# Top-32 masks that alternate between VectorE with TensorE's count and ScalarE's Sign with row sums

## The reference, cut to what matters

```python
scores = jnp.einsum('bthd,bghd->bhtg', Q, K) / np.sqrt(DH).astype(np.float32)
scores = jnp.where(vision_mask[:, None, None, :], scores, -jnp.inf)
topv, topi = jax.lax.top_k(scores, K_TOP)          # K_TOP = 32, 4 heads
probs = jax.nn.softmax(topv, axis=-1)
attn = jnp.zeros_like(scores).at[bi, hi, ti, topi].set(probs)
attn_mean = attn.mean(axis=1)                      # mean over the 4 heads
c_t = jnp.einsum('btg,bgd->btd', attn_mean, V)
```

## Time and profile before

| what | value |
|---|---|
| median of 3 runs | 3208.37 us (3207.09 to 3212.95) |
| profiled execution, its own time | 3182.96 us |
| its span | 3181.2 us |
| busy in the span: TensorE, VectorE, ScalarE, GpSimd | 2495.6, 1834.1, 1441.4, 1016.0 us |
| mean granted TensorE clock | 0.878 |
| stage of the first batch, window 1254 to 1414 us: TensorE, VectorE, ScalarE, GpSimd busy | 108.91, 135.27, 90.80, 90.65 of 160 us |

### The profile page before, as it was taken

The page is one execution under the profiler, slowest core; times in us unless marked ns, Lnnn a source line. Parts: engine busy times, 40 slices in busy tenths (PEclk is TensorE's granted clock), DMA queues, the critical chain, the costliest instruction groups (busy, mean ns, idle before and its releaser), DMA issues.

```text
span 3181.2 us, 36641 instructions
## 1 busy us (share of the span) xinstructions
PE 2495.6 (78%) x12668; PEld 1499.0 (47%) x12668; DVE 1834.1 (58%) x4565; ACT 1441.4 (45%) x2298; POOL 1016.0 (32%) x419
## 2 busy tenths in 40 slices
PE   0466698999957996668898668898669798768799
PEld 0432232223214663455476455476456476456477
DVE  8455011121231113975896975796975787794877
ACT  3033476776831223631454641454651354551254
POOL 1022000100001112640581650591560490460392
PEclk9988798999978998588999679899679899669899
DMA  1044743334151112021000011000002000002000
GB/s 56 0 161 171 127 64 67 51 67 65 47 186 35 45 43 58 1 60 43 21 1 17 28 46 58 21 1 13 30 8 96 21 1 10 27 1 96 0 1 8
DMA packets 89044, 147.35 MB, mean 46 GB/s; under 512 B 16784, under 2 KB 59408, under 8 KB 88816
## 3 DMA queue, kind: packets, MB, share of 16 engines
q1 hardware_dynamic: 81328, 135.38, 16.2%
q0 software_dynamic: 7504, 9.35, 1.6%
HBM read 121.98 MB, written 22.88 MB: 46 GB/s over the span
## 4 chain that ended last, share of the span: by engine, by line
PE 56%; DVE 23%; issue 9%; ACT 7%; DMA 3%; SPq 1%; POOL 1%; DVEq 0%; ACTq 0%; POOLq 0%
PE ps L1651 7%; PE ps L1642 6%; PE ps L1254 4%; PE ps L1265 4%; PE ps L1629 3%; DVE sb_xnT L2241 3%; PE ps L1521 3%; ACT sb_arena L917 3%; PE ps L1591 2%; PE ps L1422 2%; PE ps L1489 2%; PE ps L1441 2%; PE ps L1435 2%; PE ps L1571 2%; PE ps L1580 2%
## 5 line engine op out<-in xcount | busy, mean ns | idle before, releaser
L917 ACT ACTIVATE sb_arena<-ps 128x1024 f32<-128x1024 f32 x416 | 403.2, 1021 | 166.1 <-PE ps L1254 163.5
L2241 DVE MAX8 sb_xnT<-sb_arena 128x8 f32<-128x60 f32 (+1 forms) x1728 | 245.7, 203 | 74.6 <-ACT sb_arena L1011 74.6
L1651 PE MATMUL ps<-sb_arena 128*128 128x512 f32 x512 | 278.7, 629 | 2.7 <-ACT sb_arena L1085 2.7
L689 POOL TENSOR_TENSOR sb_arena<-sb_arena 128x1024 f32<-128x1024 f32 x96 | 227.5, 2370 | 165.0 <-DVEq L2349 153.9
L1254 PE MATMUL ps<-sb_arena 96*128 96x512 bf16 x832 | 240.8, 397 | 47.3 <-issue 33.3
L1642 PE MATMUL ps<-sb_arena 128*128 128x64 f32 x2048 | 260.2, 271 | 0.0
L1642 PEld LDWEIGHTS ps<-sb_arena 128*128 128x128 f32 x2048 | 252.2, 194 | 0.3
L1098 ACT ACTIVATE sb_arena<-ps,sb_arena 128x512 f32<-128x512 f32 x256 | 175.6, 686 | 167.5 <-DVE sb_arena L2390 166.0
L801 POOL TENSOR_TENSOR sb_arena<-sb_arena 128x1601 f32<-128x1601 f32 x56 | 175.4, 3132 | 210.3 <-DVE sb_arena L2229 210.3
L691 POOL TENSOR_TENSOR sb_arena<-sb_arena 128x1024 f32<-128x1024 f32 x84 | 227.9, 2713 | 6.6
L1265 PE MATMUL ps<-sb_arena 128*32 128x512 f32 x1664 | 227.9, 620 | 1.5 <-ACT sb_arena L917 1.5
(11 more groups left out here) (342 smaller groups left out, 4755.9 us busy)
## 6 DMA issues: line engine op xcount, KB each, us to landing
sb_arena<-in_ctxT SPq DMA_DIRECT2D x13, 1601.0 KB, 7.3
sb_arena<-k_spill SPq DMA_DIRECT2D x96, 208.0 KB, 8.0
sb_arena<-in_dft SPq DMA_DIRECT2D x5, 2048.0 KB, 8.0
k_spill<-sb_arena SPq DMA_DIRECT2D x12, 832.0 KB, 5.2
sb_arena<-in_w SPq DMA_DIRECT2D x16, 512.0 KB, 7.2
sb_arena<-in_idft SPq DMA_DIRECT2D x4, 2048.0 KB, 9.6
sb_arena<-in_wf SPq DMA_DIRECT2D x8, 1024.0 KB, 12.9
sb_arena<-q_spill SPq DMA_DIRECT2D x96, 64.0 KB, 9.2
```

The lines of the kernel that those rows point to most:

```text
L689: link(eng.tensor_tensor(heads(tmp if e else v2[:, :, hs]), src, mix, ALU.mult))
L917: A(probs0[:, 2 * (m % 4):2 * (m % 4) + 2, :], ps[:, 2 * (m % 2):2 * (m % 2) + 2, :], ACT.Exp).then_inc(pair_probs, 1)
L1651: mm(ps[:, S2_BANKS[n % 4], :], q2z[:, h, t * P:(t + 1) * P], kT2[:, h // 2, :], start=True, stop=True).then_inc(s2_done, 1)
L2241: ins = V.max(cand[:, n % 2, 8 * j:8 * j + 8], s_sb[:, n % 6, c0:c0 + w])
```

## The change

Even items stay as they are. For odd items the mask comes from ScalarE: `Sign(score + bias)` over the 1601 scores, where the bias is minus a value just under the 32nd largest. VectorE makes this bias with three instructions on one column, and no longer compares the scores. The mask is then plus and minus one, and its row sums come out of the same instruction; TensorE sums the 128 row sums with a single 128 x 1 matmul, and ScalarE copies the one number with its sign turned. `settle` and `weight` of an odd item move from step k == 4 to step k == 6 of the next item. `scale_head` takes Relu in place of Copy, so that the negative products become zero, and the last two items' masks are clipped at zero.

```diff
-ALL_DECIDED = int(np.float32(P * TOPK).view(np.int32))
+ALL_DECIDED = [int(np.float32(P * n).view(np.int32)) for n in (TOPK, GKEYS - 2 * TOPK)]
+JUST_UNDER = 2.0 ** -22
...
 # GpSimd
                     pool.wait_ge(e1_ready, nth(b, e1_ready, n + 1))
+                    if n % 2:
+                        pool.wait_ge(sign_ready, nth(b, sign_ready, n // 2 + 1))
                     pool.wait_ge(w1_ready, nth(b, w1_ready, n + 1))
                     G.tensor_tensor(e, e, kept01[:, n % 2, 0:GKEYS], ALU.mult).then_inc(p1_kept, 1)
...
 # ScalarE
-                    A(p if n % H1 else p_mean[:, t % 2, 0:GKEYS], p, ACT.Copy, scale=stat1[:, n % 3, WEIGHT:WEIGHT + 1]).then_inc(p1_scaled, 1)
+                    A(p if n % H1 else p_mean[:, t % 2, 0:GKEYS], p, ACT.Relu, scale=stat1[:, n % 3, WEIGHT:WEIGHT + 1]).then_inc(p1_scaled, 1)
...
                     A(probs1[:, n % 3, 0:GKEYS], s_sb[:, n % 6, 0:GKEYS], ACT.Exp, bias=bias).then_inc(e1_ready, 1)
-                    act.wait_ge(count_done, nth(b, count_done, n + 1))
-                    A(kept_by_col[0:1, :], ps[0:1, 7, 3 * P:4 * P], ACT.Copy, accum_out=kept[0:1, n:n + 1]).then_inc(count_ready, 1)
-                    A(top_e[:, n % 2, :], top[:, n % 2, :], ACT.Exp, bias=bias,
-                      accum_out=stat1[:, n % 3, SUM:SUM + 1]).then_inc(sum1_ready, 1)
+                    if n % 2:
+                        if n >= 3:
+                            act.wait_ge(p1_kept, nth(b, p1_kept, n - 1))
+                        A(kept01[:, 1, 0:GKEYS], s_sb[:, n % 6, 0:GKEYS], ACT.Sign, bias=under[:, 2:3], accum_out=signs).then_inc(sign_ready, 1)
+                        A(top_e[:, n % 2, :], top[:, n % 2, :], ACT.Exp, bias=bias,
+                          accum_out=stat1[:, n % 3, SUM:SUM + 1]).then_inc(sum1_ready, 1)
+                        act.wait_ge(count_done, nth(b, count_done, n + 1))
+                        A(kept[0:1, n:n + 1], ps[0:1, 7, 3 * P:3 * P + 1], ACT.Copy, scale=-1.0).then_inc(count_ready, 1)
+                    else:
...
 # TensorE, count(n)
-                    pe.wait_ge(choice_ready, nth(b, choice_ready, n + 1))
                     if n >= 1:
                         pe.wait_ge(count_ready, nth(b, count_ready, n))
+                    if n % 2:
+                        pe.wait_ge(sign_ready, nth(b, sign_ready, n // 2 + 1))
+                        ins = mm(ps[0:1, 7, 3 * P:3 * P + 1], signs, ones[:, :], start=True, stop=True)
+                    else:
...
 # VectorE
-                    with dve.If(kept_bits != ALL_DECIDED):
+                    with dve.If(kept_bits != ALL_DECIDED[n % 2]):
...
-                        if k == 4 and n >= 1:
+                        if k == (6 if (n - 1) % 2 else 4) and n >= 1:
                             settle(n - 1)
                             weight(n - 1)
                         search(n + 1, k)
...
+                    least = eights[:, TOPK - 1:TOPK]
+                    if n % 2:
+                        if n >= 3:
+                            dve.wait_ge(sign_ready, nth(b, sign_ready, n // 2))
+                        V.tensor_scalar(st[:, NEG:NEG + 1], eights[:, 0:1], -1.0, None, ALU.mult)
+                        V.tensor_scalar(under[:, 0:1], least, JUST_UNDER - 1.0, 1.0e-30, ALU.mult, ALU.add)
+                        link(V.tensor_scalar(under[:, 1:2], least, -1.0 - JUST_UNDER, None, ALU.mult))
+                        V.tensor_scalar(under[:, 2:3], under[:, 1:2], under[:, 0:1], None, ALU.max).then_inc(top_ready, 1)
+                    else:
...
+                        V.tensor_scalar(kept01[:, 0, 0:GKEYS], s, least, None, ALU.is_ge).then_inc(choice_ready, 1)
```

More of the change, by code:

```diff
@@ L244, in program @@
         kept_by_col = at(o, [P]); o += P
+        signs = at(o, [1]); o += 1
+        under = at(o, [3]); o += 3
         probs1 = at(o, [3, KS]); o += 3 * KS
@@ L445, in program @@
         sum1_ready = sem("sum1_ready", 16)
-        choice_ready = sem("choice_ready", 16)
+        choice_ready = sem("choice_ready", 8)
+        sign_ready = sem("sign_ready", 8)
         count_ready = sem("count_ready", 16)
@@ L1046, in _ @@
                     A(probs1[:, n % 3, 0:GKEYS], s_sb[:, n % 6, 0:GKEYS], ACT.Exp, bias=bias).then_inc(e1_ready, 1)
-                    act.wait_ge(count_done, nth(b, count_done, n + 1))
-                    A(kept_by_col[0:1, :], ps[0:1, 7, 3 * P:4 * P], ACT.Copy, accum_out=kept[0:1, n:n + 1]).then_inc(count_ready, 1)
-                    A(top_e[:, n % 2, :], top[:, n % 2, :], ACT.Exp, bias=bias,
-                      accum_out=stat1[:, n % 3, SUM:SUM + 1]).then_inc(sum1_ready, 1)
+                    if n % 2:
[7 more added lines that the diff above has]
+                    else:
+                        act.wait_ge(count_done, nth(b, count_done, n + 1))
+                        A(kept_by_col[0:1, :], ps[0:1, 7, 3 * P:4 * P], ACT.Copy, accum_out=kept[0:1, n:n + 1]).then_inc(count_ready, 1)
+                        A(top_e[:, n % 2, :], top[:, n % 2, :], ACT.Exp, bias=bias,
+                          accum_out=stat1[:, n % 3, SUM:SUM + 1]).then_inc(sum1_ready, 1)
                     if 1 <= n < TILES * H1 - 1:
@@ L1495, in count @@
                 def count(n):
-                    pe.wait_ge(choice_ready, nth(b, choice_ready, n + 1))
                     if n >= 1:
                         pe.wait_ge(count_ready, nth(b, count_ready, n))
[L1500 to L1503, removed]
+                    if n % 2:
+                        pe.wait_ge(sign_ready, nth(b, sign_ready, n // 2 + 1))
+                        ins = mm(ps[0:1, 7, 3 * P:3 * P + 1], signs, ones[:, :], start=True, stop=True)
+                    else:
+                        pe.wait_ge(choice_ready, nth(b, choice_ready, n // 2 + 1))
+                        for i in range(KCH):
+                            k = -i % KCH
+                            ins = mm(ps[0:1, 7, 3 * P:3 * P + KW[k]], ones_col[:, :], kept01[:, 0, k * P:k * P + KW[k]],
+                                     start=(i == 0), stop=(i == KCH - 1))
                     ins.then_inc(count_done, 1)
@@ L2266, in _ @@
                         dve.wait_ge(p1_scaled, nth(b, p1_scaled, n - 2))
[L2267 to L2271, removed]
+                    least = eights[:, TOPK - 1:TOPK]
[7 more added lines that the diff above has]
+                    else:
+                        V.tensor_scalar(st[:, NEG:NEG + 1], eights[:, 0:1], -1.0, None, ALU.mult).then_inc(top_ready, 1)
+                        if n >= 2:
+                            dve.wait_ge(p1_kept, nth(b, p1_kept, n - 1))
+                            dve.wait_ge(count_ready, nth(b, count_ready, n - 1))
+                        V.tensor_scalar(kept01[:, 0, 0:GKEYS], s, least, None, ALU.is_ge).then_inc(choice_ready, 1)
                 mean = p_mean[:, (TILES - 1) % 2, 0:GKEYS]
@@ L2279, in _ @@
                     dve.wait_ge(e1_ready, nth(b, e1_ready, n + 1))
-                    link(V.scalar_tensor_tensor(s_cut[:, 0:GKEYS], kept01[:, n % 2, 0:GKEYS], stat1[:, n % 3, WEIGHT:WEIGHT + 1],
-                                                probs1[:, n % 3, 0:GKEYS], ALU.mult, ALU.mult))
+                    link(V.scalar_tensor_tensor(s_cut[:, 0:GKEYS], kept01[:, n % 2, 0:GKEYS], 0.0, probs1[:, n % 3, 0:GKEYS], ALU.max, ALU.mult))
                     dve.wait_ge(p1_added, nth(b, p1_added, n - TILES))
-                    V.tensor_tensor(mean, mean, s_cut[:, 0:GKEYS], ALU.add).then_inc(p1_added, 1)
+                    V.scalar_tensor_tensor(mean, s_cut[:, 0:GKEYS], stat1[:, n % 3, WEIGHT:WEIGHT + 1], mean, ALU.mult, ALU.add).then_inc(p1_added, 1)
                 dve.wait_ge(p1_added, nth(b, p1_added, TILES * (H1 - 1)))
```

## The result

The changed kernel takes 3223.14 us (median, 3219.5 to 3232.17) against 3207.73 us for the kernel before, measured beside it. The ratio estimated from all runs of both is 1.0059, with a 95% interval from 1.0032 to 1.0085 (the two medians alone give 1.0048): slower by 0.6%, where I had forecast no change. The profiled execution took 3222.62 us.

A forecast was written before the change was run, and what follows sets the result against it. VectorE was taken to set the pace for most items, with a ScalarE and TensorE loop only just hidden. Per batch -2.5 + 2.5 + 1.2 - 1.45 = -0.25 us, times 4 -1 us: 3207 us, range 3187 to 3223.

The forecast's parts named there:

- the washout: Whole kernel: gains and losses cancel, -1 us, told as no change; own range 3201 to 3214 us, chance 0.40.
- rival 4: Mask by Sign inexact for some odd items, each done over: 17 us an item, 550 us for all 32; chance 0.05.
- Term a: Items 1 to 5, two pairs: VectorE's saved comparison makes each pair 1.25 us shorter, -2.5 us per batch.
- Term b: Items 5 to 7 and 9 to 11: longer ScalarE and TensorE chain, 1.2 us later each, +2.5 us per batch.
- Term c: Behind `context`, two places a batch: lower TensorE clock lengthens the scores, +0.6 us each, +1.2 us per batch.
- Term d: Items 13 to 15: no scores left, VectorE's saving counts once and the last count shortens, -1.45 us per batch.
- The later `settle` at k == 6 costs nothing: Odd items' `settle`, one step of items 1 to 5: the later place stays covered, 0.9 us to spare, price zero.
- the mask's chain to T + 4.15: Odd item: mask, sums and count done 4.15 us after its negative maximum starts (T), 0.45 us later than before.
- the scores out at T + 9.4: `score_out` for the next even item's search ends 9.4 us after the odd item's negative maximum starts; VectorE waits 0.5 us.
- Rival 3: TensorE stays at half clock through the scores behind `context`, exponentials come later: +14 us, 3222 us; chance 0.25.

The follow-up runs named there:

- Runs 2: Kernel before with only `settle` and `weight` of odd items moved from k == 4 to k == 6: ratio 1.0098 to the kernel before.
- run 4: Changed kernel, wrong-count items not done over, GpSimd's product of an odd item waiting for the next even item's comparison: ratio 0.9928 to the kernel before.
- run 6: Changed kernel with step 2**-24 and the even items' comparison in the form that also writes its sum to an accumulator: ratio 0.9937 to the kernel before.
- run 5: Kernel before with GpSimd's product of every item waiting for the next item's comparison: ratio 0.9877 to the kernel before.
- run 3: Changed kernel, wrong-count items not done over, `settle` and `weight` of odd items back at k == 4: ratio 0.9990 to the kernel before.

## Why the prediction was wrong, by its steps

**The time.** I forecast 3207 us with a range to 3223 and measured 3223.14. The likeliest case, the washout, was not what happened; rival 4 was: I had given one item done over 17 us and a chance of 0.05. One item took 18.5 us, and the stage of its batch was 20.3 us longer than with the step 2**-24 (171.0 against 150.7). The failing step is that chance. I knew the step's size, 2**-22 of a score, and that it is wide enough to take in a neighbour; with 4 x 8 odd items of 128 rows, 4096 thresholds, one such neighbour in all of them is enough for 18 us. I counted the price of each item but not the number of chances.

**Washout.** Without the item done over the ratio is 1.0005, or 1.0018 without the branch. That part of the forecast holds, but by luck: the terms cancelled in another way than I wrote. For the first batch, from the rows of before and after:

| term | predicted, us per batch | measured |
|---|---|---|
| a, items 1 to 5 | -2.5 | 0.0 (32.61 and 32.61) |
| b, to the end of counts 7 and 11 | +2.5 | +1.5 (20.4 and 20.41 against 19.63 and 19.62) |
| c, count end to `score_out` behind `context` | +1.2 | -0.4 (7.24 and 6.75 against 7.28 and 7.15) |
| d, last items | -1.45 | -0.5 |
| sum | -0.25 | +0.6 (151.2 against 150.6) |

Over all four batches, and with the run with the step 2**-24 as the kernel after, the same terms are 0.0, +1.1, +0.1 and -0.5 us per batch: a and d stay as they are, b is less than half of its forecast, and the -0.4 of term c is that of one batch. The product with the values alone takes 3.8 to 5.4 us before and 4.7 to 5.2 in that run, from place to place.

**Term a** is the step whose mechanism was wrong, and the sentence that failed is "The later `settle` at k == 6 costs nothing". I followed the later weight to GpSimd's product, and asked only who waits for the product. I didn't ask what runs beside it: the product moved from 1.9 us ahead of the comparison to 0.28 us ahead, and by so much the comparison waits longer (2.16 to 3.79 us). The saving of 1.7 us per odd item came back as a comparison 1.6 us longer in each even one. Runs 2, 4 and 6 show it from three sides: the move alone slows the kernel before, a product behind the comparison takes the wait away, and another form of the comparison does so with the product in its place. The number that misled me was the comparison's 2.16 us of the earlier trace rows, which I read as its price. Two signs were in the trace of the kernel before. In its timeline the product of item 1 and the comparison of item 2 end 0.85 us apart (1284.41 and 1285.26):

```profile
1281.19 3.22 POOL L801 TENSOR_TENSOR sb_arena<-sb_arena 128x1601 f32<-128x1601 f32 x1 [4.91 <-DVE sb_arena L2229]
...
1283.10 2.16 DVE L2271 TENSOR_SCALAR sb_arena<-sb_arena 128x1601 bf16<-128x1601 f32 x1
```

And in the comparison's group row (least, median, most) the least is half the median:

```profile
L2271 DVE TENSOR_SCALAR sb_arena<-sb_arena x64: 1041/2150/3628, 1263.0 to 2851.8; 128x1601 bf16<-128x1601 f32 x64
```

The rest of term a was right: the mask's chain to T + 4.15 (1293.92 + 0.19 is T + 4.1), the scores out at T + 9.4 (1299.94 in run 4, where T is 1290.61: T + 9.3), and a pair of 15.0 us (15.17 in run 4, 15.39 in run 6, once the comparison doesn't wait).

**Term b** has the right sign and two thirds of the size or less: 0.7 and 0.8 us a place against 1.2, both inside its bounds. I didn't separate its parts by a run, so which of them was too large stays open.

**Term c** was wrong. The clock behind `context` did not suffer: the scores there take 2.00 us at both places of all four batches, as before, although TensorE has one short count ahead of `context` instead of thirteen matmuls. VectorE's wait grew from 2.00 to 2.63 us, not to 3 to 5. In the stretch of items 1 to 6 the granted clock is 0.53, as it was. Rival 3, which rests on this, did not happen.

**Term d** gave a third of its size (from item 13's negative maximum to the start of the product behind the last count 19.11 us against 19.58). VectorE's busy time was to fall by 56 us; it rose by 11.3, of which 18.5 are the item done over. With the step 2**-24 it is 1827.9 us, only 6.2 less than before, for the profile counts a comparison that waits as busy.

## What to carry to other kernels

A duration read beside another engine is not an operation's price: look at the least of its group, and at whether its end keeps a fixed distance to the end of something on GpSimd. When an edit moves a step, follow it to each operation that it releases, and then ask what stands beside that operation at its new place, not only who waits for it. A fallback that redoes an item has a price times a number of chances; count the chances (here 4096 thresholds) before you call it unlikely.

And before a pass is moved to another engine, see whether the pass is long because it waits: one `wait_ge` on GpSimd gave 1.2% on the kernel before (run 5), about twice what this change lost.

## What the runs showed of the hardware

- VectorE's comparison of 1601 f32 scores into bf16 takes 1.05 us by itself. Beside GpSimd's product of 3.0 to 3.2 us it ends 0.85 to 0.86 us after the product in every case, before and changed, whether it starts 0.27 or 2.06 us after the product does: it takes 1.94 to 3.80 us. In the form with an accumulator it takes 1.87 us with or without GpSimd (run 6).
- GpSimd waits for VectorE in the same way: its addition over 1601 columns takes 3.02 us, and 3.76 to 4.34 us when it starts while such a comparison is under way (kernel before).
- Sign with a column as bias, 128 x 1601 from f32 to bf16, takes 1616 ns and its accumulator 186 ns (medians of 32), as long as the exponential (1.62 us).
- From the copy of the count on ScalarE to VectorE's next operation behind the register load, 0.9 us pass in run 3 (1288.28 + 0.16 to 1289.31), and the trace shows VectorE idle in them.
